# Cross-attention stack on one core: the transposes of 64 tokens in two row groups and two banks, with other places for some of them

## What is computed

```python
# grouped
q = rmsnorm(x, norm_w) @ wq
scores = einsum('btgrd,bsgd->bgrts', q, cond @ wk) / sqrt(32)
x = x + einsum('bgrts,bsgd->btgrd', softmax(scores), cond @ wv) @ wo
# masked
logits = einsum('bhqd,bhkd->bhqk', x @ Wq, ctx @ Wk) / 8 + col_bias
x = softmax(logits) @ (ctx @ Wv) @ Wo + bo + x
```

## Time and profile before

| | |
|---|---|
| median of three runs | 1509.15 us (1506.8 to 1509.26) |
| the profiled execution | 1509.95 us, its span 1508.2 us |
| PE busy | 1487.8 us (99%), 8480 matmuls |
| PE weight loads | 1232.5 us |
| DVE, POOL, ACT busy | 989.6, 912.7, 744.5 us |
| granted TensorE clock | 0.998 |
| one iteration, from the third on | about 165 us |

### The profile page before, as it was taken

The page is one execution under the profiler, slowest core; times in us unless marked ns, Lnnn a source line. Parts: engine busy times, 40 slices in busy tenths (PEclk is TensorE's granted clock), DMA queues, the critical chain, the costliest instruction groups (busy, mean ns, idle before and its releaser), DMA issues.

```text
span 1508.2 us, 23315 instructions
## 1 busy us (share of the span) xinstructions
PE 1487.8 (99%) x8480; PEld 1232.5 (82%) x8480; DVE 989.6 (66%) x1644; ACT 744.5 (49%) x1317; POOL 912.7 (61%) x825
## 2 busy tenths in 40 slices
PE   7998999999999999999999999999999999999998
PEld 7987887888778887888788877888788877887787
DVE  5676757765776657665776667565766577666764
ACT  4566576335733564346633573346533663357321
POOL 0074467557765587567756686468756775568541
PEclk9999999999999999999999999999999999999999
DMA  9999562122312231132212232143113231222101
GB/s 323 327 405 409 199 232 91 42 79 84 126 52 69 98 119 50 44 126 83 79 46 76 92 112 64 34 136 119 43 43 103 81 101 53 65 99 91 57 1 56
DMA packets 101649, 170.12 MB, mean 113 GB/s; under 512 B 17056, under 2 KB 51360, under 8 KB 95520
## 3 DMA queue, kind: packets, MB, share of 16 engines
q1 hardware_dynamic: 97552, 151.06, 30.3%
q10 hardware_dynamic: 3824, 17.04, 2.8%
q0 software_dynamic: 160, 0.53, 0.1%
HBM read 116.95 MB, written 51.65 MB: 112 GB/s over the span
## 4 chain that ended last, share of the span: by engine, by line
PE 87%; POOL 4%; DVE 3%; ACT 2%; SPq 1%; DMA 1%; issue 1%; ACTq 0%; DVEq 0%
PE OB L375 16%; PE OB L376 15%; PE OB L377 15%; PE SB L375 10%; PE SB L377 9%; PE SB L376 9%; POOL xhl L1344 4%; PE TB L507 3%; PE MX L507 3%; PE TB L543 1%; PE SB L484 1%; DMA s_fm<-prob 1%; PE OB L430 1%; PE OB L427 1%; ACT xhl L851 1%
## 5 line engine op out<-in xcount | busy, mean ns | idle before, releaser
L1315 POOL TENSOR_TENSOR prob<-prob,small 128x512 f32<-128x512 f32 x256 | 278.7, 1091 | 255.3 <-DVE small L1115 255.0
L816 ACT ACTIVATE prob<-prob 128x512 f32<-128x512 f32 x128 | 80.8, 632 | 274.2 <-DVE prob L1102 271.6
L1093 DVE SCALAR_TENSOR_TENSOR prob<-SB,aux 128x512 f32<-128x512 f32 x128 | 88.0, 688 | 182.4 <-PE SB L377 181.8
L1309 POOL TENSOR_TENSOR prob<-prob,small 128x512 f32<-128x512 f32 x128 | 136.2, 1064 | 117.3 <-DVE small L1087 117.0
L375 PE MATMUL SB<-foldM,xhl 128*128 128x512 f32 x512 | 203.9, 398 | 1.6 <-issue 0.3
L375 PE MATMUL OB<-pT,foldN 128*128 128x512 f32 x512 | 205.0, 400 | 0.0
L376 PE MATMUL OB<-pT,foldN 128*128 128x512 f32 x512 | 199.8, 390 | 0.0
L377 PE MATMUL SB<-foldM,xhl 128*128 128x512 f32 x512 | 199.7, 390 | 0.0
L377 PE MATMUL OB<-pT,foldN 128*128 128x512 f32 x512 | 199.7, 390 | 0.0
L376 PE MATMUL SB<-foldM,xhl 128*128 128x512 f32 x512 | 199.4, 389 | 0.0
L1087 DVE TENSOR_REDUCE small<-prob 128x8 f32<-128x512 f32 x128 | 87.1, 680 | 93.0 <-ACT prob L826 91.6
(11 more groups left out here) (140 smaller groups left out, 3851.4 us busy)
## 6 DMA issues: line engine op xcount, KB each, us to landing
prob<-in_wkvM_dram SPq DMA_DIRECT2D x32, 512.0 KB, 8.4
ring<-s_fm SPq DMA_DIRECT2D x64, 256.0 KB, 5.5
ring<-s_fn SPq DMA_DIRECT2D x128, 128.0 KB, 2.6
out_dram<-x ACTq DMA_DIRECT2D x15, 1024.0 KB, 3.9
s_fm<-prob SPq DMA_DIRECT2D x16, 512.0 KB, 8.4
wraw<-in_wqG_dram SPq DMA_DIRECT2D x8, 1024.0 KB, 6.8
s_fn<-x SPq DMA_DIRECT2D x16, 512.0 KB, 5.8
ring<-in_xT_dram SPq DMA_DIRECT2D x32, 256.0 KB, 3.2
```

The lines of the kernel that those rows point to most:

```text
L816: act.activation(own, own, ACT.Exp).then_inc(S["exped"], 1)
L1093: dve.scalar_tensor_tensor(out=own, in0=bank, scalar=M_SCALE, in1=row, op0=ALU.mult, op1=ALU.add).then_inc(S["biased"], 1)
L1309: pool.tensor_tensor(own, own, hmax[u % 2].unsqueeze(2).broadcast_to([P, HH, KEYS]), ALU.subtract).then_inc(S["evac"], 1)
L1315: pool.tensor_tensor(own, own, rsum[u % 2].unsqueeze(2).broadcast_to([P, HH, KEYS]), ALU.mult).then_inc(S["normed"], 1)
```

## The change

A pair of chunks (2p, 2p+1) is now transposed together, in 16 transposes of 64 tokens. Tokens 0 to 63 of each 128 (array rows 0 to 63) go to TB, tokens 64 to 127 (rows 64 to 127) to MX, in turns. Each bank then holds half of the tokens of both chunks; pt_hi and pt_lo of the two banks write them to their places in two chunks of pT or pF in pieces of 64 columns. Both semaphore increments stand on the last two transposes. product waits for both splits of its pair. pT has four buffers instead of two (place is made by dropping sqsum and spare, whose work moves to xsq, a small cst and pF), so ACT no longer waits for products (prodd is gone).

```diff
-            def transposes(it, ph, t, first, tail=False):
+            def transposes(it, ph, p, first, tail=False):
...
-                pe.wait_ge(S["normed"], 8 * (k - 1) + 4 * (t // 4) + 4)
+                pe.wait_ge(S["normed"], 8 * (k - 1) + 4 * (p // 2) + 4)
...
-                out = t_bank(ph, t)
-                for tt in range(TT):
-                    last = pe.transpose(out[:, tt * P:(tt + 1) * P], pr[:, tt, t * P:(t + 1) * P], ident[:, :])
-                last.then_inc(S["trans"], 1)
+                for c in range(2):
+                    for tt in range(TT):
+                        for r in range(2):
+                            rows = slice(64 * r, 64 * r + 64)
+                            keys = slice((2 * p + c) * P, (2 * p + c + 1) * P)
+                            cut = slice(c * 256 + tt * 64, c * 256 + tt * 64 + 64)
+                            last = pe.transpose(t_bank(r)[:, cut], pr[rows, tt, keys], ident[rows, rows])
+                            if c == 1 and tt == TT - 1:
+                                last.then_inc(S["trans"], 1)
...
             def product(it, ph, t, first, tail=False):
 
-                pe.wait_ge(S["pt_lo"], 16 * it - 8 * (ph == 0) + t + 1)
+                pe.wait_ge(S["pt_lo"], 16 * it - 8 * (ph == 0) + 2 * (t // 2) + 2)
...
-                                 pT[:, t % 2, 0, :], pT[:, t % 2, 1, :], t == 0, t == KC - 1)
+                                 pT[:, t % 4, 0, :], pT[:, t % 4, 1, :], t == 0, t == KC - 1)
...
-                for u in range(5, STEPS):
-                    scores(it, 1, u, first)
+                scores(it, 1, 5, first)
+                scores(it, 1, 6, first)
+                out_part(it, 1, 2, 0)
+                scores(it, 1, 7, first)
                 transposes(it, 2, 0, first)
+                out_part(it, 1, 3, 0)
                 transposes(it, 2, 1, first)
-                out_part(it, 1, 2, 0)
-                out_part(it, 1, 3, 0)
-                transposes(it, 2, 2, first)
-                transposes(it, 2, 3, first)
...
+                transposes(it, 3, 0, first)
                 scores(it, 2, 7, first)
-                transposes(it, 3, 0, first)
                 out_part(it, 2, 3, 0)
                 out_part(it, 2, 3, 1)
 
             def masked_masked(it, first):
 
-                transposes(it, 3, 1, first)
                 for s in range(1, STEPS):
...
-                elif not (first and ph == 0):
-                    act.wait_ge(S["sq_added"], 3 * a - 1 + c)
-                act.activation(xsq[:, c % 2, :], ring[:, c, :], ACT.Square).then_inc(S["x_sq"], 1)
+                elif not (first and ph == 0):
+                    act.wait_ge(S["qchunk"], 4 * a)
+                act.activation(xsq[:, min(c, 1), :], ring[:, c, :], ACT.Square).then_inc(S["x_sq"], 1)
```

More of the change, by code:

```diff
@@ L193, in kg_part, with pt_part, t_out @@
             return kG4[32 * r:32 * r + 32, :, :, KEYS * r:KEYS * (r + 1)].bitcast(F32), src
+        def pt_part(ph, t, part):
+            p, r = t // 2, t % 2
+            if ph in (1, 2):
+                two = pF[:, 2 * p % 4:2 * p % 4 + 2, :]
+            else:
+                two = pT[:, 2 * p % 4:2 * p % 4 + 2, part, :]
+            return two.rearrange("p c (tt r n) -> p r c tt n", r=2, n=P // 2)[:, r]
+        def t_out(t):
+            return t_bank(t)[:, :].rearrange("p (c tt n) -> p c tt n", c=2, n=P // 2)
         def fold_part(i, part):
@@ L450, in q_bound @@
                     if ph == 1 and c in (1, 2):
-                        transposes(it, 1, 2 * c - 2, first)
-                        transposes(it, 1, 2 * c - 1, first)
+                        transposes(it, 1, c - 1, first)
                     elif ph == 1 and c == DC - 1:
@@ L483, in q_bound @@
                 for tt in range(TT):
-                    last = pe.matmul(SB[1][:, tt:tt + 1], sqsum[:, tt * P:(tt + 1) * P], ones, start=True, stop=True)
+                    last = pe.matmul(SB[1][:, tt:tt + 1], xsq[:, 0, tt * P:(tt + 1) * P], ones, start=True, stop=True)
                 last.then_inc(S["qchunk"], 1)
-            def transposes(it, ph, t, first, tail=False):
+            def transposes(it, ph, p, first, tail=False):
                 k = 4 * it + ph
                 pr = prob[(ph - 1) % 2]
-                pe.wait_ge(S["normed"], 8 * (k - 1) + 4 * (t // 4) + 4)
-                if first and ph == 1 and t < 2:
-                    pe.wait_ge(S["ev_d" if t else "ev_a"], 2 * MASKED)
+                pe.wait_ge(S["normed"], 8 * (k - 1) + 4 * (p // 2) + 4)
+                if first and ph == 1 and p == 0:
+                    pe.wait_ge(S["ev_a"], 2 * MASKED)
+                    pe.wait_ge(S["ev_d"], 2 * MASKED)
@@ L542, in mixing @@
                         g = 2 * m + a
-                        last = pe.matmul(t_bank(ph, a)[32 * i:32 * i + 32, :], vG[rows, g * HD_G:(g + 1) * HD_G], pF[rows, i, :],
+                        last = pe.matmul(t_bank(a)[32 * i:32 * i + 32, :], vG[rows, g * HD_G:(g + 1) * HD_G], pF[rows, i, :],
                                          start=True, stop=True)
@@ L616, in grouped_masked @@
                     if u % 2 == 0 and u > 0:
-                        transposes(it, 0, u, False, tail)
-                        transposes(it, 0, u + 1, False, tail)
+                        transposes(it, 0, u // 2, False, tail)
                     if u > 0:
@@ L627, in grouped_grouped @@
                 scores(it, 1, 0, first)
-                transposes(it, 1, 4, first)
-                transposes(it, 1, 5, first)
+                transposes(it, 1, 2, first)
                 scores(it, 1, 1, first)
@@ L632, in grouped_grouped @@
                 scores(it, 1, 2, first)
-                transposes(it, 1, 6, first)
-                transposes(it, 1, 7, first)
+                transposes(it, 1, 3, first)
                 out_part(it, 1, 0, 1)
@@ L870, in body @@
                 for u in range(STEPS):
-                    if not first and u >= 2:
+                    if not first and u >= 2 and u % 2 == 0:
                         pt_hi(it, 0, u)
+                        pt_hi(it, 0, u + 1)
                     if not first and u == 1:
@@ L1140, in body @@
                 for u in range(STEPS):
-                    if not first and u >= 2:
+                    if not first and u >= 2 and u % 2 == 0:
                         pt_lo(it, 0, u)
+                        pt_lo(it, 0, u + 1)
                     if not first and u == STEPS - 1:
@@ L1327, in x_lo @@
                 pool.wait_ge(S["x_sq"], 4 * a + c + 1)
[L1328 to L1332 removed]
+                if c > 1:
                     pool.wait_ge(S["sq_added"], 3 * a + c - 1)
[L1334 removed]
+                pool.tensor_tensor(xsq[:, 0, :], xsq[:, 0, :], xsq[:, 1, :], ALU.add).then_inc(S["sq_added"], 1)
             def part_lo(it, i):
```

79 lines of the change are left out of this document (33 added, 46 removed).

## The result

Over 20 runs each, the changed kernel took 1510.13 us (median; 1507.94 to 1512.01) and the kernel before 1507.70 us (1505.26 to 1509.85). The ratio is 1.0013 with an interval of 1.0007 to 1.0019: slower by 2.4 us, where a change of -0.2 us, to 1509.0, had been forecast. The time is inside the range. The loss is less than the 0.2% (3 us) that the prediction took as the limit, but 20 runs resolve it. That 1509.0 lies only 1.1 us from the measured time is partly luck: the forecast started from a median of three runs, 1509.15, and the median of 20 is 1.45 lower. The change itself is off by 2.6 us.

The account below looks back on a forecast made before the run. PE was taken to bound the kernel, busy 1487.8 of 1508.2 us. Terms -5.2 - 0.5 + 2.1 + 3.4 = -0.2 us gave 1509.75 for the profiled execution, 1509.0 as median; range 1502 to 1518.

Parts of the forecast that it names:

- a group that counts: Each of 104 transpose groups that PE does not wait behind: 0.825 against 0.87 us, saving 0.05, in all -5.2 us.
- wait of transpose 5: Phase 0: PE's 0.06 to 0.07 us wait for the split of chunk 3 goes; -0.5 us in seven iterations.
- products 2 and 4 of phase 0: Each waits about 0.24 us for the second split of its pair, in seven iterations; +3.4 us in all.
- opening of phase 2: Length set by ACT, DVE and POOL until xhl is split; PE's new order there gains zero.
- opening of phase 3: DVE's split of pT leaves the chain, but PE's transposes move ahead of the scores: +0.26, times 8, +2.1 us.
- rival 3: Transpose pairs do not overlap or loads take 0.11 a step; group 1.23 us, total 1551; chance 11%.
- the two groups that I called uncounted: Two transpose groups opening phase 2 in each iteration: gain zero, since PE then waits as much longer for xhl.
- the fit without slack: Before phase 3, DVE's 0.40 us idle plus 0.825 more holds two splits of 0.61 each, without any slack.
- 1 (waits stay away): Products of phase 0 find their chunks ready and phase 3 opens without loss; 1504; chance 24%.
- 2: Pairing transposes gives the full factor of two without the drains, 0.44 a group; about 1475; chance 2%.
- 4 (pieces of 64 columns slow DVE and ACT): Writing pT in pieces costs ACT and DVE 0.2 us more each; 1518, milder forms 1512 to 1515; chance 17%.
- The forecast case: Whole kernel about unchanged, 1506.1 to 1512.1, chance 46%, with its own range 1505 to 1513.

Follow-up runs that it names:

- Part 1: Changed kernel with DVE's splits of weights in steps 1 and 3 of phase 0 put behind the following pair of pT splits: 1507.28 us, ratio 0.9990.
- Part 3: Changed kernel with the old place of phase 2's first pair (1513.62 us), or with phase 3's first pair behind the last scores (1512.45 us).
- part 2: Changed kernel with the full-height transposes of before, all places and waits kept: 1515.19 us, ratio 1.0049.
- part 5: Changed kernel with PE's new waits in phase 0 and at the openings of phases 2 and 3 attacked; several kernels, 1501.63 to 1512.09 us.
- part 4: Changed kernel with each group's transposes on rows 0 to 63 first, then 64 to 127: 1539.21 us; or each group issued twice: 1567.98 us.
- first kernel of part 5: Changed kernel with DVE's phase 0 splits reordered, an out_part moved ahead of phase 2's last scores, x of chunks 0 and 1 earlier: 1502.54 us, ratio 0.9959.
- part 5's two slow kernels: First kernel of part 5 with all four x ahead of the last scores, then also POOL's third split at phase 2's opening: 1512.09 and 1511.50 us.
- second form in part 3: Changed kernel with phase 2's first pair at its old place and its second pair one out_part earlier: 1511.51 us, ratio 1.0020.

## Why the prediction missed the loss, point by point

Stage by stage against the kernel before, per iteration, from the start times of PE's last scores matmul of each step in the two traces:

| term of the sum | predicted | measured | in all, predicted | measured |
|---|---|---|---|---|
| a group that counts | -0.050 | -0.035 | -5.2 | -3.6 |
| wait of transpose 5 | -0.07 | -0.07 | -0.5 | -0.5 |
| products 2 and 4 of phase 0 | +0.48 | +0.52 | +3.4 | +3.6 |
| opening of phase 2 | 0 | -0.01 | 0 | -0.1 |
| opening of phase 3 | +0.26 | +0.28 | +2.1 | +2.2 |
| late first copy for xhl in two iterations | not seen | +0.28 | 0 | +0.6 |
| first phase 0 and tail, beyond these terms | not seen | | 0 | +0.5 |
| sum | | | -0.2 | +2.7 |

The medians of the runs gave +2.4. Of the last term in the table, 0.2 us lie in phase 0 of the first iteration, where no transposes stand, and are not explained. The other 0.3 lie in the tail.

**Groups: mis-sized, and this is the step that failed.** It is the largest miss, 1.6 of 2.9 us; with the right size the sum would have been +1.4, a small loss, and not -0.2. The sum took 104 groups at 0.05. The prediction's own difference is 0.87 - 0.825 = 0.045, rounded up, and that alone is 0.5 us. The new group is then 0.84, not 0.825: 0.09 going in, 0.05 for the first load, seven steps of 0.063 (0.44, not 0.42), 0.15 for the last columns and the drain, 0.11 for the load behind. The old group is 0.88 by the same reckoning, not 0.87, so the difference at this place is 0.04; over the 13 groups of an iteration it is 0.02 to 0.05, 0.035 in the mean. The mechanism was as predicted: pairs 0.00 to 0.01 apart, steps near 0.06, both ends paid once. That the load sets the step, and not the 64 columns or something else, is argued and not shown: no run changed the load alone. A difference of two numbers of 0.85 that is taken 104 times wants each of its repeated terms to a thousandth.

The Trainium skill, "TensorEngine Tiling (Array Packing)", Key Properties, says that a change of the tiling mode drains TensorE; the new rows agree, 0.09 us on the way in and as much on the way out. The Trainium skill, "TensorE: Matmul & The Clock Gate", LDWEIGHTS, would give a load of 107 ns for 128 columns; in these groups loads follow each other on a row group every 0.063 us, so rival 3, which that rule makes, is refuted.

**Products of phase 0: the mechanism was right.** The waits are 0.25 and 0.24 us, forecast at 0.24, and with what follows from them in the same steps 0.52 us an iteration against 0.48. Part 1 takes just this away and gives 3.5 us. The sum forgot the tail, where the same rule holds: product 0 there waits for the second split of its pair and starts 0.94 us behind PE's last scores matmul, against 0.31 in the kernel before. After the shorter groups and a shorter end behind the last matmul, the tail is 0.19 us longer.

**Opening of phase 2: zero came out, partly by luck.** The chain of ACT, DVE and POOL does set it, but it does not hang on scores alone. Part 3 showed that the second group hangs in it too, with almost no slack: had the change made a group of both banks without moving it, 3.6 us would have come on top. And the two groups that I called uncounted do count there. From the end of scores 6 of phase 1 to that of scores 0 of phase 2 the kernel before takes 12.71 us, the new order with full-height groups (part 2) 12.92, and the changed kernel 12.70. So the new order with its waits for both banks costs 0.21, the row groups give 0.22 back, and the two cancel.

**Opening of phase 3: right, in size too.** The last scores end at 603.15 and DVE starts on them at 603.35, the same 0.20 behind as in the earlier trace rows; its second split of pT had ended at 603.21, so the fit without slack was one. From there to the second chunk of the next scores (609.95, recorded 0.50, so 610.06) are 6.91 us, forecast 6.90.

**Not seen:** in two iterations ACT starts its first copy for xhl 0.3 us late although x is ready and ACT idle. It is in the changed kernel and in those of parts 1 to 4, and not in the kernels of part 5 nor in the kernel before. Its cause stays open.

**The rivals.** 1 (waits stay away) did not come: 3.6 us of waits came in phase 0. 2 and 3 are refuted by the group of 0.84 and the step of 0.063. 4 (pieces of 64 columns slow DVE and ACT) is refuted too: DVE's splits of pT take 0.68 us and ACT's copies 0.60, as before.

**Numbers.** The forecast case came nearest, with its change off by 2.6 us; 1510.1 lies in its own range. "Faster" and "slower" had been given 0.25 and 0.30 with a limit of 0.2%, and the measured 0.13% lies inside that limit, on the slower side.

## What to carry to other kernels

When a group of small matmuls is moved to another tiling, price the group from the full matmul before it to the second full matmul behind it; the ends (here 0.34 us) are paid once, so it wants many steps in a row. Here a step saves 0.046 us (0.109 to 0.063), so eight steps only just pay for the ends. When units are fused to pairs, look at each consumer that waited for half of one: the wait for the second half is a new cost, and often, as here, one line in the order of the producing engine takes it away. Do this for the first and the last group too, which a count per iteration leaves out. When a chain is shortened by moving work on one engine, move its partners on the other engines in the same edit, or the wait comes back larger.

## What was not expected of the hardware

- Matmuls on the two row groups overlap although they are issued one group after the other: of eight and eight, three of each ran side by side (part 4), the second row group starting while three of the first had yet to start. Strict alternation was worth 0.30 us a group, not 0.50.
- DVE's split of xhl took 0.69 us where POOL was idle (first kernel of part 5) and 0.76, 1.47 or 1.77 where POOL was splitting too; POOL's took 1.29, and 1.75 where DVE's lay beside it. In each chain to xhl somebody pays this, and where it falls decides who waits.
- The same in phase 0: the changed kernel's split of weights took 0.91 us and POOL's norm beside it 1.50; in part 1, where POOL's norm (507.27 to 508.32) had ended when the split began, they took 0.68 and 1.05. DVE's splits of pT, which read one operand from a PSUM bank, took 0.68 to 0.69 beside that same norm. So the new order in part 1 did more than swap: it also moved the split of weights out of POOL's way.
- The part ahead of the first iteration took from 141.6 to 146.7 us in executions of kernels that do the same work there, twice the effect that was looked for. The traces come from several chips, but three from one chip (part 5's two slow kernels and the second form in part 3) already span 142.7 to 146.7.
